# Packed pair counts: ScalarE casts the bytes, TensorE sums out-degrees from the rows, sixteen one-hot slots

## The reference, cut to what matters

```python
edge_index = jnp.stack([src, dst])
x = _layernorm(x + _L0_gnn_ref(x, edge_index, L0_gnn_W, L0_gnn_b))
x = _layernorm(x + _L1_gnn_ref(x, src, dst, ...))       # attention over edges, 8 heads
x = _layernorm(x + _L2_gnn_ref(x, edge_index, ...))     # attention, then 3 mean-of-neighbours layers
x = _layernorm(x + _L3_gnn_ref(x, L3_gnn_weight, edge_weight1, src, dst, edge_type_16))
# inside _L0 and _L2: sums over edges, and degrees
deg = jax.ops.segment_sum(ones, row, num_segments=N)    # row = src in _L0
h = jax.ops.segment_sum(w[:, None] * x[col], row, num_segments=N)
```

## Time and profile before

| | us |
|---|---|
| median of 3 runs (lowest, highest) | 3815.69 (3813.88, 3818.88) |
| the profiled execution's own time | 3814.58 |
| its span, first to last instruction | 3812.8 |
| start of the packed count, first closing | 81.7, 158.3 |
| last closing, start of the next stage | 508.4, 541.2 |

### The profile page before, as it was taken

How to read it: one execution, slowest core, us unless ns; L and a number is a source line. 1 busy time by engine, 2 the same in 40 slices (tenths; PEclk the granted TensorE clock), 3 DMA queues, 4 the chain that set the end, 5 groups by cost and what they waited for, 6 DMA issues and landing times. The chain is left out here.

```text
span 3812.8 us, 46850 instructions
## 1 busy us (share of the span) xinstructions
PE 2943.8 (77%) x13253; PEld 2097.5 (55%) x13317; DVE 1841.9 (48%) x4590; ACT 875.8 (23%) x1237; POOL 1276.3 (33%) x929
## 2 busy tenths in 40 slices
PE   1777759774666666699999969999998999655565
PEld 1345537643555544466666658989894444344443
DVE  5999852355888887533233323434344221322223
ACT  0135644220100101022222224444441222000000
POOL 2000000007777740177667720000000000477776
PEclk9999979886677678899999989999999999778777
DMA  2046768314444421212222127666861444433334
GB/s 60 18 172 221 270 238 276 113 55 146 129 135 132 128 59 42 78 59 80 80 80 72 68 96 258 199 212 196 276 193 67 142 144 138 124 105 105 105 105 123
DMA packets 325254, 504.89 MB, mean 132 GB/s; under 512 B 27225, under 2 KB 238877, under 8 KB 317005
## 3 DMA queue, kind: packets, MB, share of 16 engines
q1 hardware_dynamic: 284477, 391.28, 30.5%
q0 software_dynamic: 40672, 112.31, 10.6%
HBM read 351.56 MB, written 152.75 MB: 132 GB/s over the span
## 5 line engine op out<-in xcount | busy, mean ns | idle before, releaser
L1791 POOL DMA_INDIRECT e7got<-rel_d,rel_i x416 | 394.6, 948 | 1139.9 <-POOLq L2699 1013.4
L1911 POOL DMA_INDIRECT a_got<-feat_d,src_i x416 | 404.1, 971 | 409.5 <-POOLq L2240 283.0
L1827 PE MATMUL e7sums<-e7got,e7hot 128*128 128x256 f32 x832 | 289.6, 508 | 197.0 <-DMA e7got<-rel_d,rel_i 166.4
L1425 PE MATMUL s_aggs<-s_blk_r,high 128*128 128x512 f32 (+1 forms) x1050 | 400.8, 382 | 20.7 <-DVE low L1544 20.5
L1425 PE MATMUL s_aggs<-s_blk_r,low 128*128 128x512 f32 (+1 forms) x1050 | 389.1, 371 | 0.0
L2740 PE MATMUL q_prods<-w,q_xt 128*128 128x512 f32 x800 | 352.8, 599 | 13.4 <-ACT q_xt L2760 13.4
L1827 PEld LDWEIGHTS e7sums<-e7got,e7hot 128*128 128x128 f32 x832 | 203.0, 255 | 280.4 <-issue 243.2
L1643 POOL TENSOR_SCALAR g_absent<-g_pairs 128x3200 bf16<-128x3200 f32 x25 | 274.8, 10992 | 171.4 <-DMA g_pairs<-pairs_d 171.3
L1690 PE MATMUL g_sums<-value,g_turned 128*128 128x257 f32 x1250 | 299.0, 383 | 8.6 <-ACT g_turned L1754 8.6
L1668 PE MATMUL g_scores<-key_t,g_q 128*128 128x512 f32 (+1 forms) x700 | 280.6, 556 | 19.9 <-DMA g_q<-query_d 13.3
L1799 DVE TENSOR_SCALAR e7hot<-iota,dloc,weight 128x128 f32<-128x128 f32 x416 | 115.7, 364 | 356.6 <-PE e7sums L1827 348.1
(11 more groups left out here) (422 smaller groups left out, 4469.7 us busy)
## 6 DMA issues: line engine op xcount, KB each, us to landing
s_blk<-turned_d SPq DMA_DIRECT2D x60, 1280.0 KB, 5.9
rel_d<-q_rows SPq DMA_DIRECT2D x25, 2048.0 KB, 7.5
s_blk<-turned_d SPq DMA_DIRECT2D x45, 960.0 KB, 5.1
pairs_d<-u_rows SPq DMA_DIRECT2D x25, 1600.0 KB, 8.1
turned_d<-u_line SPq DMA_DIRECT2D x25, 1600.0 KB, 7.1
g_pairs<-pairs_d SPq DMA_DIRECT2D x25, 1600.0 KB, 6.8
t_blk<-pairs_d SPq DMA_DIRECT2D x20, 1280.0 KB, 10.0
t_blk<-pairs_d SPq DMA_DIRECT2D x15, 960.0 KB, 5.1
```

Source lines behind the costliest of these rows:

```text
L1425: last = pe.matmul(aggs[:, idx % 2, half, 0:w], feats[l][part][:, a, half * P:(half + 1) * P], blk_r[:, q % RINGS, a % GA, 0:w], start=a = ...
L1791: pool.indirect_dma_start(got[:, j % U, :], None, table, bass.IndirectOffsetOnAxis(ap=index[:, j:j + 1], axis=0)).then_inc(arrived[j % U / ...
L1827: return pe.matmul(sums[:, 0:D], hot[:, u, :], got[:, u, :], start=False, stop=False)
L1911: pool.indirect_dma_start(got[:, n % 2, s, :], None, table, bass.IndirectOffsetOnAxis(ap=k.src_i[:, j:j + 1], axis=0)).then_inc(arrived[n ...
```

## The change

The four parts of the title, as the code has them:

- **Casts.** `apart` and `take_apart` are gone. ScalarE reads byte 0, 1 or 2 of each int32 of `whole` (a uint8 view with a step of 4) and casts it straight into `rows`. `rows` is now of type float32r, which TensorE reads in its matmuls; the transposes are ordinary matmuls against an identity of the same type.
- **Out-degrees.** `marked`, `hist` and `tally` are gone. At each closing TensorE multiplies, for each of the 7 groups, a [128, 7] matrix `marks[:, g, :]` (ones in column g) with the up to 512 columns of `rows` of the group, and adds it in `sums`: one row of sums for each group. At the end `sums` is copied out, turned by four small transposes and copied to `k.deg_src`.
- **The check.** POOL copies byte 3 of `whole` into `above` and adds it to `tops` once per tile. `heavy` is set when any top byte was above zero, or when the two degree sums of a lane differ. ScalarE waits for POOL's copy of the tile before (`topped`) before it overwrites `whole`.
- **Ring and loops.** RING is 16 slots in place of 8, the loops of VectorE and TensorE run over 16 slots, and VectorE has no words to load and no branches.

```diff
-    LOOK = 2
-    RING = 4 * LOOK
+    FOURS = 4
+    RING = 4 * FOURS
...
-        apart = sb("apart", [P, 3, THIRD], I32)
-        rows = sb("rows", [P, NP])
+        rows = sb("rows", [P, NP], F32R)
-        largest, flag = sb("largest", [P, 2]), sb("flag", [1, 2])
-        marked = sb("marked", [EP, 2, 4, P + T], BF16)
-        hist = c.enter_context(nc.psum_tensor("u_hist", [P, 512], F32))
+        tops, above, top = sb("tops", [P, THIRD]), sb("above", [P, THIRD]), sb("top", [P, 1])
+        wrong, degrees, flag = sb("wrong", [P, 2]), sb("degrees", [P, 2]), sb("flag", [1, 2])
+        ident_r, marks = sb("ident_r", [P, P], F32R), sb("marks", [P, FLIPS, FLIPS], F32R)
+        given = sb("given", [FLIPS, 512])
+        sums = c.enter_context(nc.psum_tensor("u_sums", [P, 512], F32))
...
-            pool.memset(rows[:], 0.0).then_inc(ready, 1)
+            pool.memset(rows[:].bitcast(F32), 0.0).then_inc(cleared, 1)
+            pool.memset(tops[:], 0.0).then_inc(summed, 1)
+            pool.wait_ge(summed, 1)
+            for t in range(T):
+                pool.wait_ge(copied, (t + 2) * COPIES)
+                if t >= 1:
+                    pool.wait_ge(summed, t + 1)
+                pool.tensor_copy(above[:], whole[:].bitcast(U8)[:, 3:4 * THIRD:4]).then_inc(topped, 1)
+                pool.wait_ge(topped, t + 1)
+                pool.tensor_tensor(tops[:], tops[:], above[:], ALU.add).then_inc(summed, 1)
...
-            dve.wait_ge(ready, 4)
-
-            def marks(i, b):
-                dve.wait_ge(tallied, i + 1)
-                dve.tensor_tensor(marked[:, b, :, 0:P], k.iota_b[0:EP, :].unsqueeze(1).broadcast_to([EP, 4, P]),
-                                  cols(k.slo, i * 4, 4).unsqueeze(2).broadcast_to([EP, 4, P]), ALU.is_equal).then_inc(hot, 1)
-                dve.tensor_tensor(marked[:, b, :, P:P + T], k.iota_b[0:EP, 0:T].unsqueeze(1).broadcast_to([EP, 4, T]),
-                                  cols(k.shi, i * 4, 4).unsqueeze(2).broadcast_to([EP, 4, T]), ALU.is_equal).then_inc(hot, 1)
-
-            def take_apart(t):
-                dve.wait_ge(copied, t * COPIES + 2 * COPIES)
-                dve.sem_inc(k.passed, 1)
-                dve.wait_ge(spread_out, t * 3 + 3)
-                dve.sem_inc(k.passed, 1)
-                dve.tensor_single_scalar(apart[:, 0, :], whole[:], 255, ALU.bitwise_and).then_inc(parted, 1)
-                dve.tensor_scalar(apart[:, 1, :], whole[:], 8, 255, ALU.arith_shift_right, ALU.bitwise_and).then_inc(parted, 1)
-                dve.tensor_single_scalar(apart[:, 2, :], whole[:], 16, ALU.arith_shift_right).then_inc(parted, 1)
-
-            def closings(group):
-                word = load_word(dve, k, group)
-                with dve.If((word & 15) != 0):
-                    for u in range(4):
-                        with dve.If(turn_here(word, u) != 0):
-                            take_apart(tile_before(word, u))
-
-            def eight(i, closing):
-                for u in range(8):
-                    j = i * 8 + u
-                    if u % 4 == 0:
-                        if closing:
-                            closings((i * 2 + u // 4 - LOOK))
-                        marks(2 * i + u // 4, u // 4)
+            step(dve.tensor_copy(ident_r[:], k.ident[:]))
+            step(dve.tensor_copy(marks[:].rearrange("p g m -> p (g m)"), k.zero[:, 0:1].broadcast_to([P, FLIPS * FLIPS])))
+            step(dve.tensor_copy(marks[:].rearrange("p g m -> p (g m)")[:, 0:FLIPS * FLIPS:FLIPS + 1],
+                                 k.ones[:, 0:FLIPS]))
+            dve.sem_inc(marked, 1)
+            dve.wait_ge(ready, 3)
+
+            with dve.Fori(0, S // RING) as i:
+                for u in range(RING):
+                    j = i * RING + u
                     dve.wait_ge(used, j + 1)
                     dve.tensor_scalar(hot_d[:, u, :], k.iota_b[:], cols(k.dloc, j, 1), None, ALU.is_equal).then_inc(made, 1)
                     dve.tensor_scalar(hot_s[:, u, 0:THIRD], places[:], cols(column, j, 1), cols(value, j, 1),
                                       ALU.is_equal, ALU.mult).then_inc(made, 1)
-
-            eight(0, False)
-            with dve.Fori(1, S // 8) as i:
-                eight(i, True)
-            for group in range(S // 4 - LOOK, S // 4):
-                closings(group)
-            take_apart(T - 1)
             dve.wait_ge(final, 1)
-            step(dve.tensor_copy(k.deg_src[:], hist[:, 0:T]))
-            step(dve.tensor_reduce(largest[:, 0:1], k.deg_dst[:], AX.X, ALU.max))
-            step(dve.tensor_reduce(largest[:, 1:2], k.deg_src[:], AX.X, ALU.max))
-            dve.sem_inc(reduced, 1)
-            dve.wait_ge(laid, 1)
-            step(dve.tensor_reduce(flag[:, 0:1], hist[0:1, P:2 * P], AX.X, ALU.max))
-            step(dve.tensor_reduce(flag[:, 1:2], hist[0:1, 2 * P:3 * P], AX.X, ALU.max))
-            step(dve.tensor_tensor(flag[:, 0:1], flag[:, 0:1], flag[:, 1:2], ALU.min))
-            step(dve.tensor_scalar(flag[:, 0:1], flag[:, 0:1], 255.5, None, ALU.is_gt))
+            step(dve.tensor_copy(given[:], sums[0:FLIPS, :]))
+            dve.sem_inc(given_in, 1)
+            dve.wait_ge(upright, 1)
+            by_group = counts[:, 1, 0:4 * FLIPS].rearrange("p (a g) -> p g a", a=4)
+            step(dve.tensor_copy(k.deg_src[:, 0:4 * (FLIPS - 1)].rearrange("p (g a) -> p g a", a=4), by_group[:, 0:FLIPS - 1, :]))
+            step(dve.tensor_copy(k.deg_src[:, 4 * (FLIPS - 1):T], by_group[:, FLIPS - 1, 0:T - 4 * (FLIPS - 1)]))
+
+
+            dve.wait_ge(summed, T + 1)
+            step(dve.tensor_reduce(top[:], tops[:], AX.X, ALU.max))
+            step(dve.tensor_scalar(wrong[:, 0:1], top[:], 0.5, None, ALU.is_gt))
+            step(dve.tensor_reduce(degrees[:, 0:1], k.deg_dst[:], AX.X, ALU.add))
+            step(dve.tensor_reduce(degrees[:, 1:2], k.deg_src[:], AX.X, ALU.add))
+            step(dve.tensor_tensor(wrong[:, 1:2], degrees[:, 0:1], degrees[:, 1:2], ALU.subtract))
+            dve.sem_inc(checked, 1)
+            dve.wait_ge(added, 1)
+            step(dve.tensor_copy(flag[:], counts[0:1, 0, 0:2]))
+            step(dve.tensor_tensor(flag[:], flag[:], flag[:], ALU.mult))
+            step(dve.tensor_reduce(flag[:, 0:1], flag[:], AX.X, ALU.max))
+            step(dve.tensor_scalar(flag[:, 0:1], flag[:, 0:1], 0.5, None, ALU.is_gt))
             step(dve.tensor_copy(k.heavy[:], flag[:, 0:1]))
...
-            pe.sem_inc(tallied, 2)
-            pe.wait_ge(ready, 4)
+            pe.wait_ge(ready, 3)
...
-            pe.matmul(hist[:, 0:T], zero[0:EP, 0:P], zero[0:EP, 0:T], start=True, stop=False)
+            pe.matmul(sums[0:FLIPS, :], zero[:, 0:FLIPS], zero[:, 0:512], start=True, stop=False)
+            pe.wait_ge(marked, 1)
             def flip(closing, g):
                 pe.wait_ge(lined, closing * FLIPS + flip_room(g))
                 pe.sem_inc(k.passed, 1)
+                w = min(4, T - 4 * g) * P
+                pe.matmul(sums[0:FLIPS, 0:w], marks[:, g, :], rows[:, 4 * g * P:4 * g * P + w], start=False, stop=False)
                 for a in range(4 * g, min(T, 4 * g + 4)):
-                    last = pe.transpose(flips[:, g % 4, (a % 4) * P:(a % 4 + 1) * P], rows[:, a * P:(a + 1) * P], k.ident[:])
+                    last = pe.matmul(flips[:, g % 4, (a % 4) * P:(a % 4 + 1) * P], rows[:, a * P:(a + 1) * P], ident_r[:],
+                                     start=True, stop=True)
                 last.then_inc(flipped, 1)
-            def tally(i, b):
-                pe.wait_ge(hot, 2 * i + 2)
-                for u in range(4):
-                    last = pe.matmul(hist[:, 0:T], marked[:, b, u, 0:P], marked[:, b, u, P:P + T], start=False, stop=False)
-                last.then_inc(tallied, 1)
-
             def four(i, b):
-                tally(i, b)
...
-            with pe.Fori(0, S // 8) as i:
-                four(2 * i, 0)
-                four(2 * i + 1, 1)
-            pe.matmul(hist[:, 0:T], zero[0:EP, 0:P], zero[0:EP, 0:T], start=False, stop=True).then_inc(final, 1)
+            with pe.Fori(0, S // RING) as i:
+                for b in range(FOURS):
+                    four(FOURS * i + b, b)
             for n in range(BANKS):
                 end(n).then_inc(full, 1)
             for closing in (T - 1, T):
                 pe.wait_ge(spread_out, closing * 3 + 3)
                 for g in range(FLIPS):
                     flip(closing, g)
-            pe.wait_ge(reduced, 1)
-            pe.transpose(hist[0:1, P:2 * P], largest[:, 0:1], k.ident[:])
-            pe.transpose(hist[0:1, 2 * P:3 * P], largest[:, 1:2], k.ident[:]).then_inc(laid, 1)
+            pe.matmul(sums[0:FLIPS, :], zero[:, 0:FLIPS], zero[:, 0:512], start=False, stop=True).then_inc(final, 1)
+            pe.wait_ge(given_in, 1)
+            pe.wait_ge(copied, (T + 1) * COPIES)
+            for a in range(4):
+                last = pe.transpose(counts[:, 1, a * FLIPS:(a + 1) * FLIPS], given[:, a * P:(a + 1) * P], k.ident[0:FLIPS, 0:FLIPS])
```

(33 more changed lines are left out.)

## The result

The changed kernel takes 4223.8 us (median; 4214.6 to 4230.7) against 3817.2 before on the same chip: 1.1065 times as long, interval [1.1041, 1.1089]. The forecast was 3776, and the measured time lies far outside its range of 3757 to 3812. The profiled execution took 4221.3 us, its span is 4219.5.

The account below looks back on a forecast made before the run. The prediction took VectorE as the bound, with the DMA engines sharing it in late tiles. Gains of 18.5 (first closing) and 23.4 (tiles) less 2.5 (end) made 39.4 us: forecast 3776 us, range 3757 to 3812.

Parts of the forecast that it names:

- Part 5: Ring of 16 slots: a closing, nine slots of VectorE, no longer stops it; no gain by itself.
- Part 1: VectorE without marks and `take_apart`: 0.625 us a slot, first closing at 139.8 instead of 158.3, gain 18.5 us.
- the four rivals: POOL not holding VectorE 3768 (0.17), POOL's upper price 3801 (0.14), store floor 3789 (0.13), dearer hold 3839 (0.12).
- The slower rival: POOL and VectorE also wait for each other at hand-overs, 7.5 us a tile: 3839 us, chance 0.12.
- the sum: Per tile the larger of VectorE with POOL and TensorE: 326.5 us against 349.9, gain 23.4; in all 39.4.
- last closing to the next stage: Stage's end: seven sums between the last transposes at a lower clock, charged 2.5 us.
- Part 2: POOL's two instructions per tile hold VectorE for their whole time: copy 2.0, addition 2.26 us.
- P: POOL's time per tile, charged to VectorE: 4.3 us, ends 3.3 and 5.9.
- the first rival: POOL doesn't hold VectorE, so every tile is TensorE's: 7.7 us less, 3768 us, chance 0.17.
- Part 3: TensorE loses `tally`, gains seven sums (1.6 us) per closing: a tile of s slots costs 0.45·s + 7.0 us.
- Part 4: ScalarE's three byte casts stay at 3.0 us; the store of `rows` stays a floor of 8.6 to 11.6 a tile.
- the third rival: The store of `rows` is the floor in the last 14 tiles: 12 to 14 us more, 3789 us, chance 0.13.

Follow-up runs that it names:

- e4: The kernel before, with only TensorE's loop body doubled to 16 slots (1571 instructions): 4215.8 us, ratio 1.1040.
- e1: The whole change, but with the ring and both loops at 8 slots again (881 instructions in TensorE's body): 3799.2 us, ratio 0.9950.
- e8: The change with ring and loops of 16, but transposes and sums once behind each four slots (899 instructions): 3828.1 us, ratio 1.0041.
- after: The changed kernel itself, with ring and loops of 16 (1759 instructions in TensorE's body), against the kernel before: 4223.8 us, ratio 1.1065.
- e11: e8 with the transposes and sums once per two slots instead of once per four (1207 instructions): 3854.4 us, ratio 1.0113 to the kernel before.
- e12: e6 with the transposes and sums once per four slots, behind them (451 instructions in TensorE's body): 3837.3 us, ratio 1.0070.
- e6: e1 without GpSimd's copies and additions, the heaviness test as in the kernel before: 3791.8 us, ratio 0.9945.
- e7: The kernel before, only with ScalarE's casts from bytes and without `take_apart`: 3811.0 us, ratio 0.9993.
- e2: The change with its ring of 16, but TensorE's body 8 slots long (995 instructions) with computed ring addresses: 4021.7 us, ratio 1.0535.
- e14: e8 with the transposes back inside the slots in three of its four groups of four (1544 instructions): 4182.0 us, ratio 1.0957 to the kernel before.
- e13: The kernel before with 900 never-run matmuls between the halves of TensorE's loop body (2593 instructions listed, 793 can run): 3865.7 us, ratio 1.0133.
- e5: The kernel before with 380 never-run matmuls behind both halves of TensorE's loop body (1553 instructions listed, 793 can run): 3867.8 us, ratio 1.0142.
- e10: The kernel before with the word load and branch of e5, but one never-run matmul instead of 380: 3863.1 us, ratio 1.0136.
- e9: The kernel before with 380 never-run matmuls between the halves of TensorE's loop body (1553 instructions listed): 3859.1 us, ratio 1.0125.

## Why the prediction was wrong

**The step that failed is Part 5**, "ring of 16 ... Gain: none by itself", and with it the sentence "twelve matmuls (four slots) take 1.79 us, 0.45 us a slot" in Part 1 as TensorE's price. Both take the 16 places as an edit of a buffer. In the code the constant is also the length of the loops, and TensorE's body holds a closing for every slot. I priced what is executed, and left out what has to be there to be executed. The one sentence that named it, "in every case but one where loop code stalls", had neither price nor chance; the four rivals were all about engines. What the runs showed in its place: the doubled body of TensorE's loop is read again in every pass, 15.4 us a pass, 26 passes, 401.6 us; e4 shows that the doubling alone does it, and e1 and e8, with shorter bodies, do not have the loss. The slower rival with its 3839 us had the right sign and the wrong mechanism.

**The rest of the sum**, read from e1, which is the change without the long body (only with a ring of 8, which the prediction did not price):

| term | forecast | e1 |
|---|---|---|
| first closing (158.3 before) | 139.8 | 144.9 |
| from there to the last closing (350.0 before) | 326.5 | 336.1 |
| last closing to the next stage (32.8 before) | +2.5 | +2.6 |
| gain at the start of the next stage | 39.4 | 24.7 |

- *Part 1.* 0.625 us a slot is right: in after, where VectorE runs freely, 119.06, 119.69, 120.31. The first closing is 5 us late; in e8, e11 and e12, whose closings stand behind the slots, it is at 141.2, 140.6 and 140.4. That the long jumps over a closing cost these 5 us fits, but wasn't measured by itself.
- *Part 2.* POOL's copy takes 1.05 us (forecast 2.0), its addition 2.41 (2.26): P = 3.5 instead of 4.3. The hold exists, as e1's rows show: a `hot_d` of 0.25 us lasts 1.28 and ends with POOL's addition. It isn't added to VectorE's work, as the sum did, but lies mostly in a wait for TensorE. Taking POOL away starts the next stage 2.8 us earlier (513.63 in e6, 516.45 in e1); the first rival had 7.7.
- *Part 3.* Late tiles of e1 are 11.6 us apart (forecast 11.1 to 12.0 for 9 to 11 slots). The six early tiles took 116.7 us (forecast 111.4), the other eighteen 219.4 (215.1). The sum gave the early ones to VectorE alone; in e1, 145 to 262 us, the two engines wait for each other in turn:

```profile
DVE u_hot_d L786 <- PE u_counts L826: 21.0, 11, 3.7
...
PE u_counts L826 <- DVE u_hot_d L786: 16.1, 24, 1.4
```

  With a ring of 8 the prices partly add where the sum took the larger of the two. That this is the whole of the 9.6 us is my reading, without a run of its own.
- *Part 4.* Right. The casts from bytes take what those from words took (1068 ns in e1, 1081 before):

```profile
L929 ACT CAST u_rows<-u_whole 128x1042 fp32r<-128x1042 uint8 x75 | 74.8, 1068 | 8.6 <-DMA pairs_d<-u_rows 8.6
```

  The wait for the store of `rows` is 8.6 us in all, as it was before (8.2), and 4.3 in after: no new floor, and the third rival falls. e7 shows that this part alone changes nothing (0.9993): VectorE's 46 us less (25 times 1.84) are not on the path in this kernel.
- *Later stages.* e1 gains 24.7 us at the next stage and 16.4 in the span, e6 27.6 and 29.1, after loses 401.6 and 406.7. The differences of 5 and 8 us behind the stage are no larger than those between runs of one kernel (e1: 3793.5 to 3801.7; e6's profiled run was its fastest), and I read nothing from them.

What stays open: how many of the machine's own instructions a listed one is, which jumped-over code counts, and so where the limit lies exactly; and what sixteen places would be worth with early flips and a short body, since e2 and e8 each paid for their short body in another way.

## What to carry to other kernels

Where an edit doubles an unrolled loop body, count the instructions that can run in it (here it was TensorE's), and look at the instruction queue's packets: here they rose from 54 to 277, 8.6 for each of 26 passes, as the code was read again each time. In these runs that began between 1207 and 1544 listed instructions (e11, e14), and in the change it cost 15 us a pass. A body of 8 slots avoided it, with a ring of 8 for nothing (e1), with a ring of 16 at the price of computed addresses (e2, 5% slower); taking the rarely run code out of each slot avoided it too (e8). An "issue" wait on an engine with full input buffers doesn't say by itself that the code is read again: TensorE's loads have 265 us of it in e2 with 55 packets, and 368 in after with 277. The packets tell the two apart.

## What the runs showed of the hardware

- A TensorE loop of 1544 to 1759 runnable instructions is read again in every pass, on average 7.8 to 8.8 packets of 16.4 KB each (e14 256, after 277, e4 283 packets against 54, over 26 passes); one of 1207 is not (e11, 55 packets).
- A block of up to 1800 instructions in one piece that is never run adds two or three packets (e13 56, e5 57, against 54), while closings that are jumped over are read along: 27 packets in three passes without a closing (after).
- One more word load and branch in TensorE's loop costs 1 us a pass (e10: 3863.1 against 3809.0 over 52 passes), and about as much with 760 instructions to jump over as with two (e9: 3859.1 against 3809.0).
- Matmuls whose addresses are computed mostly start a slot of three every 0.62 us instead of 0.45 (e2, 423 to 425 us, at a granted clock of 1.00), with further gaps of 1.6 and 2.6 us before a group of four slots there.
- GpSimd's copy of every fourth byte takes 1.05 us for 1042 elements, 1.01 ns each; its memset in the earlier trace rows had 0.93.
